# Row sums and squares of the last two norms: from VectorE's statistics to accumulator outputs

## The reference, cut to what matters

```python
x = _layernorm(x + L0(x, edge_index))      # mean of neighbours, two layers
x = _layernorm(x + L1(x, edge_weight))     # three hops
x = _layernorm(x + L2(x))                  # products along edges
x = _layernorm(x + L3(x, edge_index))      # attention
# the end of L3:
mu = jnp.mean(out, axis=-1, keepdims=True)
var = jnp.mean(jnp.square(out - mu), axis=-1, keepdims=True)
return ln_gamma * (out - mu) * jax.lax.rsqrt(var + LN_EPS) + ln_beta
# and around it:
m = jnp.mean(x, axis=axis, keepdims=True)
v = jnp.var(x, axis=axis, keepdims=True)
return (x - m) / jnp.sqrt(v + eps)
```

## Time and profile before

| | |
|---|---|
| median of 3 runs | 2902.57 us (2900.96 to 2903.87) |
| profiled execution | 2898.8 us, of it the span of the trace 2896.7 us |
| busy share of the span | PE 77%, weight loads 52%, DVE 51%, POOL 42%, ACT 23% |

### The profile page before, as it was taken

How to read it: one execution, slowest core, us unless ns; L and a number is a source line. 1 busy time by engine, 2 the same in 40 slices (tenths; PEclk the granted TensorE clock), 3 DMA queues, 4 the chain that set the end, 5 groups by cost and what they waited for, 6 DMA issues and landing times.

```text
span 2896.7 us, 31032 instructions
## 1 busy us (share of the span) xinstructions
PE 2220.1 (77%) x8708; PEld 1498.8 (52%) x8708; DVE 1490.0 (51%) x4063; ACT 663.0 (23%) x1371; POOL 1216.4 (42%) x1733
## 2 busy tenths in 40 slices
PE   4677798999989869999999999999923535353550
PEld 2444798447775435655556555677712424243430
DVE  8999676556860010340105302455534757575768
ACT  3777654114540000100002000355400000000002
POOL 0000278888888800010000000001048888888850
PEclk8888999999999979999999999999956666666675
DMA  6565688443455234454445433433243333333321
GB/s 238 241 258 218 235 282 265 147 161 115 127 175 157 76 125 155 149 206 151 132 155 183 154 118 122 113 98 101 79 76 94 99 94 98 93 97 94 95 69 44
DMA packets 191911, 411.95 MB, mean 142 GB/s; under 512 B 47734, under 2 KB 131409, under 8 KB 191761
## 3 DMA queue, kind: packets, MB, share of 16 engines
q1 hardware_dynamic: 128276, 240.65, 26.3%
q10 hardware_dynamic: 27325, 102.15, 9.8%
q0 software_dynamic: 36160, 67.34, 8.5%
HBM read 326.06 MB, written 83.96 MB: 142 GB/s over the span
## 4 chain that ended last, share of the span: by engine, by line
PE 54%; POOL 18%; DVE 18%; issue 4%; DMA 4%; ACT 1%; SPq 0%; ACTq 0%; DVEq 0%; POOLq 0%
PE banks L1509 24%; POOL row_ring L2141 10%; PE banks L933 8%; DVE features_and_rows L567 6%; POOL spare_count L338 5%; PE banks L1059 4%; POOL table_dense_weights L789 4%; PE banks L1176 3%; PE banks L1191 3%; PE banks L2363 3%; DVE pair_and_bias_rows L564 2%; PE banks L1496 2%; PE banks L1949 1%; PE banks L1479 1%; PE banks L1966 1%
## 5 line engine op out<-in xcount | busy, mean ns | idle before, releaser
L789 POOL DMA_INDIRECT table_dense_weights<-pair_weight,dst x416 | 416.9, 1002 | 424.5 <-DVE weights_c L828 317.3
L1509 PE MATMUL banks<-own_term,features_and_rows 128*128 128x391 f32 (+1 forms) x1656 | 554.7, 492 | 38.4 <-DMA own_term<-table_dense_weights 38.4
L1509 PEld LDWEIGHTS banks<-own_term,features_and_rows 128*128 128x128 f32 x1656 | 313.2, 190 | 266.6 <-issue 40.9
L2141 POOL DMA_INDIRECT row_ring<-table_heads,src x416 | 408.1, 981 | 83.4 <-issue 65.6
L1535 DVE TENSOR_SCALAR features_and_rows<-banks,hop_bias 128x391 f32<-128x391 f32 (+1 forms) x24 | 15.0, 625 | 645.6 <-PE banks L1509 645.6
L933 PE MATMUL banks<-split_rows,count_columns 128*128 128x512 f32 x1200 | 310.8, 406 | 3.3 <-ACT count_columns L915 3.3
L1509 PE MATMUL banks<-features_and_rows 128*128 128x391 f32 (+1 forms) x840 | 282.4, 491 | 0.0
L338 POOL IOTA spare_count<- 128x256 int32 x728 | 263.8, 362 | 7.2
L2363 PE MATMUL banks<-row_ring,edge_to_window 128*128 x880 | 237.9, 434 | 16.9 <-DVE edge_to_window L2338 13.5
L933 PEld LDWEIGHTS banks<-split_rows,count_columns 128*128 128x128 f32 x1200 | 222.5, 189 | 53.0 <-issue 5.3
L585 PE MATMUL banks<-features_and_rows,pair_and_bias_rows 128*128 128x400 f16 x806 | 182.4, 384 | 86.9 <-DVE features_and_rows L567 52.8
(11 more groups left out here) (423 smaller groups left out, 3078.1 us busy)
## 6 DMA issues: line engine op xcount, KB each, us to landing
hidden<-table_counts SPq DMA_DIRECT2D x305, 160.0 KB
table_dense_weights<-weights_c ACTq DMA_DIRECT2D x26, 1600.0 KB, 5.7
own_term<-table_dense_weights SPq DMA_DIRECT2D x52, 782.0 KB
own_term<-table_dense_weights SPq DMA_DIRECT2D x34, 780.5 KB
pair_and_bias_rows<-table_edge_rows ACTq DMA_DIRECT2D x50, 512.0 KB
weights_c<-table_edge_rows ACTq DMA_DIRECT2D x50, 512.0 KB
features_and_rows<-table_dense_weights SPq DMA_DIRECT2D x26, 782.0 KB
table_counts<-hidden SPq DMA_DIRECT2D x25, 800.0 KB, 3.4
```

Source lines behind the costliest of these rows:

```text
L789: e.indirect_dma_start(out=self.table, out_offset=bass.IndirectOffsetOnAxis(ap=self.place[:, t:t + 1], axis=0), in_=self.values[:, t:t + 1 ...
L1509: m = e.matmul(psum[b][:, 0:wide], z_block(block)[:, f * P:(f + 1) * P], streamed[tile % STREAM][:, lo - from_column:lo - from_column + wi ...
L2141: e.indirect_dma_start(out=ring_rows[:, ring_at(t), 0:ATT_ROW], out_offset=None, in_=t_h, in_offset=bass.IndirectOffsetOnAxis(ap=src[:, t: ...
```

## The change

The multiplication in `attended` becomes a `scalar_tensor_tensor` that also writes out the row's sum, and so does the residual addition of `inner_norm`. `centred_root` takes the place of `mean_and_root` in both norms: one DVE instruction turns the group's sums into minus the means, ACT squares each row with that as its bias and sums up the squares by its own accumulator output, and ACT's root takes the sum times 1/256 plus eps. The squares themselves are written to four buffers in `start_cut` and never read. The mean is then added with its sign turned, the shift in `store` is a product of two columns, and the stages are emitted in another order: `inner_stats`, `inner_norm`, `attended`, `store`, with the same distances.

```diff
-                t = V(lambda e, n=n, j=j: e.tensor_tensor(heads(spare[:, j, :]), sums_of[:, n, :, 0:HEAD_DIM],
-                                                          a_dst[:, j, :].unsqueeze(2).broadcast_to([P, HEADS, HEAD_DIM]), ALU.mult),
+                t = V(lambda e, n=n, j=j: e.scalar_tensor_tensor(
+                    out=heads(spare[:, j, :]), in0=sums_of[:, n, :, 0:HEAD_DIM], scalar=1.0,
+                    in1=a_dst[:, j, :].unsqueeze(2).broadcast_to([P, HEADS, HEAD_DIM]), op0=ALU.mult, op1=ALU.mult,
+                    accum_out=stats[:, j, 0:1]),
                       t if j == g[0] else None, (s_owned, g[0] // TILES_AT_ONCE + 1), merged(383))
...
+        of_norm = lambda k, g: tiles(stats, g)[:, :, k]
+        squares_at = [at[:, n * DIM:(n + 1) * DIM] for at in start_cut for n in range(2)]
+        squared_by = []
+
+        def centred_root(rows_of, g, k, summed):
+            centred = V(lambda e: e.tensor_scalar(of_norm(k + 1, g), of_norm(k, g), -1.0 / DIM, None, ALU.mult), summed)
+            for j in g:
+                before = squared_by[-len(squares_at)] if len(squared_by) >= len(squares_at) else None
+                t = A(lambda e, j=j, to=squares_at[len(squared_by) % len(squares_at)]: e.activation(
+                    to, rows_of(j), ACT.Square, bias=stats[:, j, k + 1:k + 2], accum_out=stats[:, j, k + 2:k + 3]), centred, before)
+                squared_by.append(t)
+            return A(lambda e: e.activation(tiles(rstd, g), of_norm(k + 2, g), ACT.Sqrt, bias=eps[:, 0:1], scale=1.0 / DIM), t)
+
         def inner_stats(g):
-            roots[g] = mean_and_root(lambda j: spare[:, j, :], g, weighed[g])
+            roots[g] = centred_root(lambda j: spare[:, j, :], g, 0, weighed[g])
 
         def inner_norm(g):
...
-                t = V(lambda e, j=j: e.scalar_tensor_tensor(out=spare[:, j, :], in0=spare[:, j, :], scalar=mv[:, j, 0:1],
-                                                            in1=brow[:, B_GAMMA, :], op0=ALU.subtract, op1=ALU.mult), r)
+                t = V(lambda e, j=j: e.scalar_tensor_tensor(out=spare[:, j, :], in0=spare[:, j, :], scalar=stats[:, j, 1:2],
+                                                            in1=brow[:, B_GAMMA, :], op0=ALU.add, op1=ALU.mult), r)
             for j in g:
                 t2 = V(lambda e, j=j: e.scalar_tensor_tensor(out=x[:, j, :], in0=spare[:, j, :], scalar=rstd[:, j:j + 1],
-                                                             in1=x[:, j, :], op0=ALU.mult, op1=ALU.add), t)
-            roots[g] = mean_and_root(lambda j: x[:, j, :], g, t2)
+                                                             in1=x[:, j, :], op0=ALU.mult, op1=ALU.add, accum_out=stats[:, j, 3:4]), t)
+            roots[g] = centred_root(lambda j: x[:, j, :], g, 3, t2)
...
-            shift = V(lambda e: e.scalar_tensor_tensor(out=tiles(sq, g), in0=tiles(mv, g)[:, :, 0], scalar=-1.0,
-                                                       in1=tiles(rstd, g), op0=ALU.mult, op1=ALU.mult), r)
+            shift = V(lambda e: e.tensor_tensor(tiles(sq, g), of_norm(4, g), tiles(rstd, g), ALU.mult), r)
...
-        in_groups(attended, inner_stats, inner_norm, store)
+        in_order((1, inner_stats), (2, inner_norm), (0, attended), (3, store))
```

## The result

The changed kernel took 2881.45 us (median of 4 runs, 2873.87 to 2883.44) against 2902.39 us before (median of 4, one run more than in the table above): a ratio of 0.9923, 95% interval 0.9904 to 0.9942, so 17 to 28 us less. It is faster, as forecast, but by more than the 13.0 us of the sum, and it lies at the lowest end of the range, which began at 2881 us. The profiled execution took 2880.86 us, 17.9 us less than the one before; its span is 2879.0 us.

The account below looks back on a forecast made before the run. VectorE bounds the last stage now; after the change ScalarE would, at 7.46 us a period against 6.07. ScalarE's terms ended at 2878.3 against 2891.6; gain 13.0 us, profiled 2885.8, plus 3.8 to the median: 2889.6 us, range 2881 to 2897.

Parts of the forecast that it names:

- the 13.0 us of the sum: Whole last stage on ScalarE: its terms end the last scaling 13.3 us earlier, less 0.3 for the outputs.
- table load: Root's table on ScalarE: one load of 1.3 us, exposed behind the first four squares; the other end was 0.
- the branch that had 60%: Last stage: ScalarE bounds at 0.45 to 0.74 us a square, gains from 5.8 to 18 us; chance 60%.
- first square after the first L2397: ScalarE's start in the last stage: first square at 2828.0, after VectorE's read, mean and two hand-overs.
- 50 squares: ScalarE, both norms: 50 squares with bias and row sum at 0.60 us each, 30.0 us.
- 25 scalings: ScalarE, last stage: 25 scalings at 0.50 us each, 13.0 us as busy now.
- idle on ScalarE: Ramp-up: ScalarE waits for group 0's second sums, 1.1 us, and 0.3 one step later, 1.4 us.
- the price of the accumulator read: Behind each square on ScalarE: 0.20 us, taken from a one-column activation, laid end to end on 0.40.
- The offset between profile and median: Whole kernel: the 3.8 us between profiled run and median carried over, from 2885.8 to 2889.6 us.
- The end after the last scaling: Output transfers: 5.1 us remain, plus 0.3 (0 to 0.7) as the last two outputs are issued closer together.
- the hidden read: Rival: ScalarE's accumulator read is hidden, squares take 0.40 to 0.45 us, VectorE bounds; 2882.7 us, chance 20%.
- Table swaps: Rival: square not in the root's table, 27 more loads on ScalarE, about 2923 us, 20 us slower; chance 5%.

## Why the prediction was too cautious, step by step
The mechanism was right: VectorE's stream shrinks to 6.1 us a period (6.07 forecast), ScalarE takes the bound, one table load stands behind the fourth square, and the stage is a sum on ScalarE. A square's pitch of 0.49 us lies in the branch that had 60%. From the stage's start, that sum against the trace, where measured terms go from start to start, so that overlap is not counted twice:

| term | forecast, us | measured, us |
|---|---|---|
| first square after the first L2397 | 6.9 | 6.8 |
| 50 squares | 30.0 (0.60 each) | 24.6 (0.49 each) |
| 14 roots | 4.6 | 4.8 |
| 25 scalings | 13.0 | 12.4 |
| table load | 1.3 | 1.3 |
| idle on ScalarE | 1.4 | 2.9 |
| stage | 57.2 | 52.8 |

**The step that failed is the price of the accumulator read.** "The read's own shape, laid end to end since it must wait for the last sum" gave 0.20 us on top of 0.40. The size of one read was right, 0.19 us; the end-to-end part was not. The next square starts 0.10 us before the read is over, so the read costs 0.09; the run without it has a pitch of 0.40. That is 50 x 0.11 = 5.5 us. Activations overlap their successors in the rows of before already: two scaled copies of 0.50 us take 0.89 us together. I had taken that overlap off the square and not off the read. Nor was it taken off the scalings: 13.0 us is the sum of their durations, and from start to start they take 12.4. The Trainium skill's page "ScalarE: Activation LUTs", section "What ACT_TABLE_LOAD costs", says that back-to-back activations overlap by about 93 ns; it does not name the read. An estimate that lets the read overlap by as much, 0.187 - 0.093 = 0.094 us, agrees with the 0.09 us measured.

**A part came back as idle time.** With shorter squares ScalarE is sooner through with the second group, and waits longer for the first group's outer sums, which hang on VectorE: 1.6 us, not 1.1. One step later it is 1.2, not 0.3. Together the terms make the 4.4 us between 57.2 and 52.8.

**The offset between profile and median** was the second error. I added the 3.8 us by which the first profiled execution lay below the median. The changed kernel's profiled run lies 0.6 us below its median, so the difference did not carry over. Of the 8.1 us between 2889.6 and 2881.45, 4.9 stand between the profiled executions (2885.8 and 2880.86; 4.0 of them from the stage to the end of the span, 0.7 from a stage that began that much earlier) and 3.2 are this.

The remaining steps. The end after the last scaling grew from 5.1 to 5.8 us, of which SP waits 5.1 for the outputs (4.3 before); I had 5.4:
```profile
SPq L166 <- DMA out<-x_nodes: 5.1, 1, 5.1
```
VectorE was forecast to idle 1.4 us in every period; it ran ahead instead, and idled 6.2 us in all, mostly at the end. Of the rivals, the hidden read was half true: 0.09 of 0.19 us remain. That the time of 2882.7 given for that case is so close to the 2881.45 measured is luck. Its stage, 50.3 us (2821.08 to 2871.4), is what the run without the read took, 50.4; the changed kernel's is 2.4 us longer, and the 3.2 us of the offset make up for that. Table swaps did not happen: the changed kernel has one load in the stage, behind the fourth square, and squares and roots alternate after it.
```profile
2829.12 0.18 ACT L2416 ACTIVATION_READ_ACCUMULATOR src_lo_onehot<-attended_rows,ln_stats 128x1 f32 x1
2829.32 1.28 ACT L2419 ACT_TABLE_LOAD   x1
2830.62 0.30 ACT L2419 ACTIVATE ln_rstd<-ln_stats,eps 128x4 f32<-128x4 f32 x1
```
The drain of 1.38 us that the Trainium skill ("ScalarE: Activation LUTs", "What ACT_TABLE_LOAD costs") adds to a load is not seen in these rows either: the load starts 0.02 us after the read before it ends, it ends at 2830.60, and the root starts at 2830.62. Moving the load out of the stage saved 1.3 us, the load's own time.

## What to carry to other kernels
Where one engine is saturated and another sleeps, price the moved work by its pitch on the new engine, helper instructions included, and make the sum for each engine: here the longer one was the new period, 6.56 us against 6.1. Moving work across engines adds hand-overs, so the order of the stages may have to be changed with it; here the same instructions in the old order left both engines waiting for each other, with a period of 8.6 us and a third of the gain. Measure such a change by the length of the stage it touches when the stages before it spread by more than the change is worth.

## What was not expected of the hardware
ScalarE's accumulator read is 0.19 us long and adds 0.09 us to the pitch; VectorE's is 0.08 long and adds 0.01 (rows of L828; the pitch of L2401 is 0.35 with it and 0.34 without, though its operation changed as well). The table that holds the exponential also serves the squares, and so does the root's: the four squares of the first group run under the one, the other 46 under the other, and between them stands one load.
